# Issuing the matmuls of two accumulation groups by turns in a transformer layer kernel bound by TensorE

## The reference

```python
k = x @ W_lat + b_lat                                   # 512 x 128 for each sequence
q = (x @ W_d + b_d).reshape(B, T, 16, 128).transpose(0, 2, 1, 3)
att = softmax(where(causal, q @ k.T / sqrt(128), -inf)) # for each of 16 heads
y = att @ k                                             # "the values": k again
x = layernorm(x + y.reshape(B, T, 2048) @ W_proj + b_proj)   # "the projection"
# router: top 256 of 512 tokens; gelu(sel @ w1 + b1) @ w2 + b2, gated, added back; layernorm
```

## Time and profile before

| | |
|---|---|
| time, median of 3 runs | 281.28 us (281.27 to 281.34) |
| profiled execution, its own time | 281.42 us |
| its span | 279.7 us |
| granted TensorE clock, mean | 0.993 of full |
| busy: TensorE matmuls / weight loads | 271.9 us / 247.3 us |
| busy: VectorE / ScalarE / GpSimd | 219.6 / 212.1 / 154.1 us |

### The profile page before, as it was taken

The page is one execution under the profiler, slowest core; times in us unless marked ns, Lnnn a source line. Parts: engine busy times, 40 slices in busy tenths (PEclk is TensorE's granted clock), DMA queues, the critical chain, the costliest instruction groups (busy, mean ns, idle before and its releaser), DMA issues.

```text
span 279.7 us, 6208 instructions
## 1 busy us (share of the span) xinstructions
PE 271.9 (97%) x1885; PEld 247.3 (88%) x1885; DVE 219.6 (79%) x702; ACT 212.1 (76%) x578; POOL 154.1 (55%) x214
## 2 busy tenths in 40 slices
PE   8999999999999999999999999999999999999991
PEld 4878999999999998999999999999999999999990
DVE  2698777777777777788789888899988888779782
ACT  3689877777777778887797777787777777878471
POOL 6458444444443346555566866665657847247652
PEclk9999999999999999999999999999999999999997
DMA  6483111011101111111111111110112200020151
GB/s 187 134 300 116 39 40 33 26 34 38 35 25 33 38 39 38 40 38 42 38 38 40 38 41 38 39 40 19 41 38 77 78 21 21 1 76 1 58 170 38
DMA packets 18843, 15.53 MB, mean 56 GB/s; under 512 B 1642, under 2 KB 18179, under 8 KB 18819
## 3 DMA queue, kind: packets, MB, share of 16 engines
q1 hardware_dynamic: 18242, 13.65, 16.5%
q0 software_dynamic: 576, 1.58, 1.6%
HBM read 12.60 MB, written 2.63 MB: 54 GB/s over the span
## 4 chain that ended last, share of the span: by engine, by line
PE 96%; DVE 2%; issue 1%; POOLq 0%; ACT 0%; DVEq 0%
PE bank L412 20%; PE bank L414 19%; PE bank L413 19%; PE bank L547 8%; PE ps_out L412 7%; PE ps_out L413 6%; PE ps_out L414 6%; PE bank L527 3%; PE bank L637 3%; PE bank L470 1%; PE bank L424 1%; DVE beats L1254 1%; POOLq L60 0%; PE bank L676 0%; DVE lost L1261 0%
## 5 line engine op out<-in xcount | busy, mean ns | idle before, releaser
L841 ACT ACTIVATE probs<-probs,negmax 128x512 f32<-128x512 f32 (+3 forms) x128 | 72.6, 576 | 5.8 <-DVE negmax L1026 4.4
L1385 POOL TENSOR_TENSOR wd_hi<-wd_raw,zero 128x256 fp32r<-128x256 f32 x31 | 23.8, 767 | 87.9 <-DVE probs L1098 84.8
L849 ACT CAST pT_hi<-bank 128x512 fp32r<-128x512 f32 (+2 forms) x96 | 43.4, 488 | 28.1 <-PE bank L547 27.7
L1026 DVE CUSTOM_DVE_ANT_0 probs<-bank,mask_row 128x512 f32<-128x512 f32 (+3 forms) x128 | 59.2, 482 | 0.7 <-PE bank L504 0.7
L1035 DVE TENSOR_TENSOR pT_lo<-bank,pT_hi 128x512 fp32r<-128x512 f32 (+2 forms) x96 | 52.9, 553 | 6.1 <-ACT pT_hi L849 5.4
L547 PEld LDWEIGHTS bank<-ident_r,prob_words 128*128 128x128 f32 x310 | 33.0, 140 | 5.4 <-ACT probs L893 0.4
L412 PE MATMUL ps_out<-wp_hi,yT_hi 128*128 128x256 f32 x124 | 37.1, 299 | 0.0
L412 PE MATMUL bank<-kT_hi,qT_hi 128*128 128x256 f32 (+2 forms) x94 | 36.5, 388 | 0.0
L413 PE MATMUL ps_out<-wp_lo,yT_hi 128*128 128x256 f32 x124 | 35.0, 282 | 0.0
L414 PE MATMUL ps_out<-wp_hi,yT_lo 128*128 128x256 f32 x124 | 35.0, 282 | 0.0
L1055 DVE TENSOR_TENSOR yT_lo<-bank,yT_hi 128x512 fp32r<-128x512 f32 x31 | 21.4, 690 | 15.8 <-PE bank L414 14.2
(11 more groups left out here) (203 smaller groups left out, 733.2 us busy)
## 6 DMA issues: line engine op xcount, KB each, us to landing
wd_raw<-in_L_attn_W_d SPq DMA_DIRECT2D x32, 128.0 KB, 2.2
wp_raw<-in_L_attn_W_proj SPq DMA_DIRECT2D x32, 128.0 KB, 2.0
wf_raw<-in_L_ffn_w SPq DMA_DIRECT2D x2, 1024.0 KB, 7.6
x_nat<-in_L_attn_x SPq DMA_DIRECT2D x4, 256.0 KB, 3.0
out<-z_all SPq DMA_DIRECT2D x4, 256.0 KB, 2.2
picked<-ranked SPq DMA_DIRECT2D x2, 258.0 KB, 2.8
wlat_raw<-in_L_attn_W_lat SPq DMA_DIRECT2D x1, 128.0 KB, 3.1
bproj_all<-in_L_attn_b_proj SPq DMA_DIRECT2D x1, 128.0 KB, 3.6
```

The lines of the kernel that those rows point to most:

```text
L841: act.activation(p_tile(s, j), p_tile(s, j), ACT.Exp, bias=negmax[:, s, j:j + 1], scale=-1.0, accum_out=sums[:, s, j:j + 1]).then_inc(exp_ ...
L849: act.copy(pT_hi[:, dst], src).then_inc(pt_hi_done, 1)
L1026: dve.tensor_tensor_reduce(p_tile(s, j), score_bank[j], mask_row[:, (TILES - 1 - j) * P:], -SCALE, -MASKED, ALU.add, ALU.min, accum_out=ne ...
L1385: pool.tensor_tensor(hi, src, nothing, ALU.add).then_inc(hi_done, 1)
```

## The change

The 29 periods that have both a projection and queries to issue (2 to 30) call a new function, which issues the same 22 matmuls in another order: one of the projection, one of the values. The waits that `values` had at its head now stand at the head of the whole. The three matmuls of tile 2 of the projection stand without partners, since the values have nine such matmuls and the projection twelve. Operands, sizes, banks and the number of instructions stay.

```diff
+            def project_and_values(at):
+                b, s = at.batch(-2), at.place(-2)
...
+                wait(pe, wp_split, at.p - 1)
+                wait(pe, y_lo_done, at.p - 1)
...
+                if at.fixed == AT_PICKED:
+                    pe.wait_ge(xs_split[0], CH)
+                if at.fixed == AT_K:
+                    pe.wait_ge(k_split, 2)
+
+                def of_projection(j, term):
+                    t = slice(j * P, (j + 1) * P)
+                    if b and head == 0 and j % 2 == 0 and term == 0:
+                        pe.wait_ge(x_seeded, j // 2 + 1)
+                    left, right = ((y_hi, wp_hi), (y_hi, wp_lo), (y_lo, wp_hi))[term]
+                    return pe.matmul(ps_out[:, j, :], left[:, t], right[s][:, :],
...
+                def of_values(i, term):
+                    if term == 0:
+                        wait(pe, pt_lo_done, at.p * 3 - 2 + i)
+                    n = (TILES - i) * P
...
+                    return pe.matmul(ps_y[:, SEQ - n:], left[vb][:, i, :], right[:, t],
...
+                for i in range(TILES - 1):
+                    for term in range(3):
+                        of_projection(i, term)
+                        of_values(i, term) if i < 2 else None
+                for term in range(3):
+                    last = of_projection(TILES - 1, term)
+                    if term == 2:
+                        last.then_inc(proj_done, 1)
+                    of_values(2, term)
+                wait(pe, pt_last_done, at.p)
+                pe.matmul(ps_y[:, SEQ - P:], k_last[vb][:, :], pT_last[:, :], ...
...
-                        project(at)
+                        project_and_values(at)
...
-                if at.live(-1):
+                if at.live(-1) and not (at.live(1) and at.live(-2)):
                     values(at)
```

More of the change, by code:

```diff
@@ L617, in project @@
                         last.then_inc(proj_done, 1)
+            def project_and_values(at):
+                b, s = at.batch(-2), at.place(-2)
+                y_hi, y_lo = yT_of(at)
+                head = at.fixed - 2 - b * HEADS
+                wait(pe, wp_split, at.p - 1)
+                wait(pe, y_lo_done, at.p - 1)
+                first = b == 0 and head == 0
+                if first:
+                    pe.wait_ge(k_split, 1)
+                    pe.wait_ge(kT_done, BATCH)
+                vb = at.batch(-1)
+                if at.fixed - 1 == vb * HEADS:
+                    pe.wait_ge(k_split, vb + 1)
+                    pe.wait_ge(k_last_done, vb + 1)
+                if at.fixed == AT_PICKED:
[8 more added lines that the diff above has]
+                    return pe.matmul(ps_out[:, j, :], left[:, t], right[s][:, :],
+                                     start=(first and j % 2 == 0 and term == 0),
+                                     stop=(head == HEADS - 1 and term == 2), skip_group_check=True)
+                def of_values(i, term):
+                    if term == 0:
+                        wait(pe, pt_lo_done, at.p * 3 - 2 + i)
+                    n = (TILES - i) * P
+                    t = slice(PT_OFF[i], PT_OFF[i] + n)
+                    left, right = ((k_hi, pT_hi), (k_hi, pT_lo), (k_lo, pT_hi))[term]
+                    return pe.matmul(ps_y[:, SEQ - n:], left[vb][:, i, :], right[:, t],
+                                     start=(i == 0 and term == 0), stop=False, skip_group_check=True)
+                for i in range(TILES - 1):
[8 more added lines that the diff above has]
+                wait(pe, pt_last_done, at.p)
+                pe.matmul(ps_y[:, SEQ - P:], k_last[vb][:, :], pT_last[:, :], start=False, stop=True,
+                          skip_group_check=True).then_inc(y_ready, 1)
```

## The result

| | before | after |
|---|---|---|
| median | 281.28 us (5 runs, 281.06 to 281.39) | 282.32 us (5 runs, 282.04 to 282.65) |
| ratio, after to before | | 1.0035 (95% interval 1.0025 to 1.0045) |
| span of the profiled execution | 279.7 us | 280.6 us |
| its own time | 281.42 us | 282.32 us |

The change made the kernel 1.04 us slower; 281.9 us with a range of 281.0 to 283.3 was forecast. The page of the changed kernel, beside the earlier trace rows, shows the same counts for every engine and nearly the same busy times. It has 6179 instructions where there were 6208, so their number did not stay: the 29 that are gone are separate wait instructions in TensorE's queue, one for each changed period.

The account below looks back on a forecast made before the run. TensorE, busy 97% of the span, was taken as the bound; 0.48 + 0.13 + 0.03 = +0.64 us took the profiled 281.42 to 282.06, or 281.9 us against the median of 281.28 (+0.23%), range 281.0 to 283.3.

Parts of the forecast that it names:

- TensorE is dense, so reordering can't gain: Projection and values stretch, 3.07 us: each matmul costs its columns, nothing is idle that the new order could fill.
- xs_lo in period 30: Wait moved ahead of period 30's projection: a start 0.43 to 0.48 us late, taken as 0.48.
- the 0.09 of period 31: Period 31: a matmul starts 0.09 us after its low part ends; the lower bound for release of the moved waits.
- k_lo in period 14: Wait moved ahead of period 14's projection: a start 0.08 to 0.13 us late, taken as 0.13.
- One sign that I named: Period 14's projection starts about 0.1 us late, with idle time ahead that names VectorE.
- The same matmuls in another order: The 22 matmuls of 29 stretches, 435 more bank changes: taken as nothing, bounds -1.3 to +2.6 us.
- the 6 ns of the first scores: First scores, five matmuls with four bank changes: at most 6 ns more per change, giving the +2.6 us bound.
- the -3 ns of the gather: Gather, eight 256-column matmuls with the bank changing at every second: 3 ns less per change, giving the -1.3 us bound.
- Turn 2: Low part of turn 2, needed 2.48 us behind the projection's start: +0.03 us for periods 18 and 25, bounds 0 to 0.16.
- proj_done later: proj_done moves from the twelfth matmul to the twentieth, 1.45 us later; its followers wait on later things, so no cost.
- the clock stays: Granted clock stays 1.00; the rival, a fall to the 1.2 GHz level, meant +89 us, chance 0.01.
- The sum: Whole kernel: 0.48 + 0.13 + 0.03 = +0.64 us, once and not in each period.

Follow-up runs that it names:

- early turn 2: Changed kernel with periods 14 and 30 in the old order and the values' 256-column matmuls paired with projection tile 2, needed 0.36 us earlier: 285.16 us, ratio 1.0140.
- order only: Changed kernel with the old order and old waits in periods 14 and 30 only, the other 27 periods by turns: 281.73 us, ratio 1.0012.

## Why the prediction was right, point by point

- **TensorE is dense, so reordering can't gain**: right. No order of the 22 matmuls that was tried was faster, and the steady stretch is 3.07 us in both.
- **xs_lo in period 30, +0.48**: measured 0.48, and **k_lo in period 14, +0.13**: measured 0.13. Both starts come 0.14 behind VectorE, the value taken from the gather and not the 0.09 of period 31. The reason that I gave, an idle TensorE, isn't shown: in period 18 of early turn 2 TensorE's last matmul had ended too (147.46 + 0.28 = 147.74), and the start came 0.06 behind VectorE. The kernel with these waits alone has +0.63 in time, where they should give 0.61. One sign that I named did not show: period 14 has no idle time that names VectorE.
- **The same matmuls in another order, 0**: the term that was mis-sized. It is +0.33 to +0.36, inside the bounds of -1.3 to +2.6. The reason that I gave for these bounds was wrong, though: the 6 ns of the first scores and the -3 ns of the gather were read as prices of a change of the bank, and two kernels show that a change of the bank costs nothing that can be measured. Nor is the streaming of the 22 matmuls the place: two thirds of the term lie behind them, in work that I took as unchanged, and why is open.
- **Turn 2, +0.03**: nothing that can be seen in the changed kernel. In period 25 its low part ends 2.27 behind the projection's start (197.40 + 0.41 - 195.54) and the matmul starts at 2.47, on time. Early turn 2 puts the price of a narrow miss at 0.10 for the next matmul, near the 0.08 that I took from the earlier trace rows.
- **proj_done later, 0; the clock stays**: nothing on TensorE's list of waits names a follower of proj_done, and the granted clock is 1.00 in period 20.
- **The sum**, +0.64, was 0.4 short of the 1.04 measured, nearly all of it by the term that I took as nothing. The verdict of slower by over 0.2% rested on 0.08 us of margin in the forecast and came out clear, 0.35%. That it came out so clear is luck: the waits alone, the part that was foreseen, have 0.26% with an interval from 0.16%.

## What to carry to other kernels

Before interleaving two dense groups, read the distance from start to start for each size: where it is proportional to the columns, as here, there is nothing to hide, and none of the orders tried here gained. What an interleaving does change is which waits stand ahead of what; list each wait that moves up, and compare the end of its releaser with the new place, period by period, since the odd periods (here two of 29) hold most of the loss. Putting the merged code back into its old order in just those two periods saves most of the loss: that is the kernel order only, with +0.36 us in place of +1.04. And sum the parts that were not touched as well: a third of the loss in the attention is not at the moved waits, and most of that third lay behind the reordered matmuls.

## What the hardware showed unexpectedly

- A change of the PSUM bank at every matmul has no price that shows: 119.8 ns for 256 columns against 119.6 with one bank, over 46 and 47 steps.
- A matmul whose operand is released only about when it is due starts on time, and the next one comes 0.10 us late (0.22 in place of 0.12). The list of waits of the matmuls shows nothing of it.
- Reordering six unlike matmuls inside one bank, all released early, cost 0.012 us in each stretch (0.27 us in the medians over 29 periods). No run here tells why.
- Behind a stretch in the new order the same scores, turns and queries took 4.26 us in place of 4.25, in five kernels besides the changed one's own; in the kernel order only, 4.25 again behind period 14, which has the old order. No run here tells why.
